# Graph layers with routed experts: the set-up taken by pairs of graphs, with identity products ahead of it on TensorE

## The chip, the cores and the metric

The kernel runs on one core of a Trainium2 chip. The metric is the device time of one execution, in microseconds (us); lower is better. The names of the engines are those of the profile: PE is TensorE, PEld its weight loads, DVE is VectorE, ACT is ScalarE, POOL is GpSimd; SPq and ACTq are the queues from which SyncE and ScalarE issue DMA transfers.

## What is computed

```python
# x: (128, 128, 256), adj: (128, 128, 128), float32: 128 graphs of 128 nodes
def gnn(X, A):                       # X = layernorm(x), A = adj
    Xw = X @ Wv + bv
    sj, si = Xw @ aw[:d, 0], Xw @ aw[d:, 0]
    e = leaky_relu(sj[:, None, :] + si[:, :, None] + ab[0], 0.2)
    alpha = A * exp(e)
    T = alpha / (alpha.sum(-1) + 1e-12)
    return relu(X @ Wk[0] + T @ (X @ Wk[1]) + T @ T @ (X @ Wk[2]) + bk.sum(0))
x = x + gnn(layernorm(x), adj)
x = x + experts(layernorm(x))        # top-1 of 16 experts, capacity 1228, times the route's probability
```

The kernel never forms `Xw`: it folds the attention vectors into the weights. `WvT` times `aw` gives two columns (`attention columns`) that stand beside `Wk[0]`, and `bv` times `aw` gives two constants. One product of a graph with the widened matrix then gives the first hop and both attention sums.

## The kernel before

One step of the main loop is a turn, and turn k works on graph k; the graphs come in batches of four (G = 4). All engines run the same turns, each with its own `slot_fn(it, k)` (POOL L472, ACT L597, DVE L771, PE L1296), written out by hand and tied together by semaphores. Work on other graphs is laid into a turn: the layer norm of the input leads (`LEAD_STATS` = 7: VectorE takes the statistics of graph k + 7 and the moments of graph k + 6; `LEAD_X0` = 2: GpSimd makes the normed graph k + 2; `LEAD_XT` = 1: TensorE transposes graph k + 1), and the residual sum, the routing and the storing lag by 2 to 10 turns. Later turns also carry tiles of the experts. Products are made in three parts of a split float32 (high by high, high by low, low by high), so each operand needs a rounded copy (`..h`, made by ACT with CAST) and a remainder (`..l`, made by DVE with a subtraction).

What a graph needs before its turn can run: statistics and moments (`st`, `mv`, DVE L913, L918), the negated mean and the variance plus epsilon (`nm`, `ve`, ACT L640, L641), the reciprocal root (`r`, POOL L479), the normed graph (`x0`, POOL L483), its transpose (`ps_xt`, PE L1321), its high part (`xth`, ACT L606) and its low part (`xtl`, DVE L810). Then PE multiplies it with `w12` (two hops, 512 columns, into `ps_z12`) and with `w0` (260 columns, the attention sums among them, into `ps_z0`). DVE adds the constants (`svs`, L839), PE spreads one column over the partitions (L1363), ACT takes two exponentials (`e`, L627, L628), DVE takes their maximum (`em`, L887), multiplies with the adjacency and divides (`al`, `ri`, `tm`), and PE transposes the result in the next turn (L1338).

The order of the set-up is this:

- SP issues the input of graphs 0 to 3 as one transfer of 512 KB (L371), then `WvT`, `aw`, `bv`, `ab` (L372 to L375, all on the semaphore `d_v`), and then the next inputs and constants. ACT issues `Wk`.
- DVE takes statistics and moments of graphs 0 to 3, spreads `bv` over a tile (`bvb`, L1216), makes the remainder of `w12` (`remainders`), the low part of graph 0, and then in `attention_columns` (L741) the columns, the constants, the high and low parts of `w0` and the vector `cvec` that `svs` adds. After that come the statistics of graphs 4 to 6 and turn 0, then `hop_biases` (L755).
- ACT forms `nm` and `ve` once per batch of four, and then the high part of `w12` (L699).
- POOL builds the constants (the identity `ident` at L460 among them) and runs its turns from -2 on.
- PE waits for `d_v`, makes the attention columns (L1287), runs turn -1 (the transposes of graph 0), makes the constants (L1481), signals both with one semaphore (`s_pe0`), and starts turn 0.

`fillers(n)` (L1486) issues n products of the identity with itself into a bank that nobody reads. Here it is called only between the last turns and the expert tiles that follow.

## Time and profile before

| | |
|---|---|
| Time of three runs, median (lowest to highest) | 757.88 us (757.74 to 757.92) |
| The profiled execution: its own time | 759.5 us |
| The profiled execution: span of the core in the trace | 757.7 us |
| Busy in that span: PE | 710.1 us (94%) |
| Busy in that span: DVE | 640.3 us (85%) |
| Busy in that span: ACT | 480.2 us (63%) |
| Busy in that span: POOL | 445.4 us (59%) |
| Mean granted clock of TensorE, as the records give it | 0.987 of full speed |

All durations of single instructions come from the profiled execution. Its time is 1.6 us above the median of the three runs; its span leaves out what lies around the instructions. A row of the timeline gives the start of an instruction in us from the span's start, its length, engine, line, operation, output and inputs, shape and number of instructions, and in brackets how long the engine had been idle and what ended the wait. The rows of PE overlap: the end of a product is modelled, so the rate of a stream is read from one start to the next.

### The profile page before, as it was taken

How to read it: one execution, taken by the hardware profiler on the slowest of the kernel's cores; microseconds unless marked ns; L12 is line 12 of the kernel's file. 1: busy time of each engine (PE TensorE's matmuls, PEld its weight loads, DVE VectorE, ACT ScalarE, POOL GpSimd, SP SyncE). 2: the span in 40 equal slices, each digit the busy share in tenths (PEclk: the TensorE clock that was granted, in tenths of full speed). 3: DMA queues.
4: the chain of work that ended last, by engine and by line, in shares of the span. 5: the costliest groups of instructions: out<-in, count | busy, mean ns of one | idle time of the engine just before them, and what ended most of it. 6: DMA issues, size and time to landing. Idle time of an engine off the chain costs nothing.

```text
span 757.7 us, 18479 instructions
## 1 busy us (share of the span) xinstructions
PE 710.1 (94%) x4815; PEld 628.7 (83%) x4815; DVE 640.3 (85%) x3101; ACT 480.2 (63%) x1506; POOL 445.4 (59%) x525
## 2 busy tenths in 40 slices
PE   4999999999999999999999999999999999958773
PEld 3888888789899998989998999999999989847662
DVE  4899999999889988989898899889898888776552
ACT  2567777666666666667666666666676676544551
POOL 4325555546666667666656666676666665665563
PEclk9999999999999999999999999999999999988997
DMA  9524444534443444444444433444443322354430
GB/s 271 143 78 135 128 130 154 166 105 148 150 128 122 131 152 155 144 151 148 135 132 152 134 117 124 149 149 143 142 141 125 117 91 85 102 156 134 122 95 1
DMA packets 92985, 100.12 MB, mean 132 GB/s; under 512 B 10379, under 2 KB 85192, under 8 KB 92882
## 3 DMA queue, kind: packets, MB, share of 16 engines
q1 hardware_dynamic: 76996, 65.96, 29.3%
q0 software_dynamic: 13008, 30.07, 10.8%
q10 hardware_dynamic: 2880, 2.92, 1.4%
q8 instruction: 43, 0.70, 0.4%
q14 instruction: 58, 0.48, 0.2%
HBM read 49.92 MB, written 54.72 MB: 138 GB/s over the span
## 4 chain that ended last, share of the span: by engine, by line
PE 85%; DVE 8%; issue 3%; another core or an unknown queue 1%; POOL 1%; DMA 1%; ACT 1%; POOLq 0%; DVEq 0%
PE ps_z12a L1291 11%; PE ps_z12b L1291 11%; PE ps_lgb L1291 9%; PE ps_z0b L1291 8%; PE ps_z0a L1291 8%; PE ps_lga L1402 5%; PE ps_z0a L1370 4%; PE ps_z0b L1370 4%; PE ps_xt L1321 4%; PE ps_z12b L1349 4%; PE ps_xt L1389 3%; PE ps_z12a L1349 3%; PE ps_lgb L1431 3%; PE ps_t L1363 2%; PE ps_t L1338 2%
## 5 line engine op out<-in xcount | busy, mean ns | idle before, releaser
L541 POOL DMA_INDIRECT out<-lent,tok x143 | 146.5, 1025 | 159.9 <-DVE lent L1203 136.4
L528 POOL DMA_INDIRECT rowbuf<-rows,idx x128 | 129.7, 1013 | 54.4 <-issue 30.3
L606 ACT CAST xth<-ps_xt 128x256 fp32r<-128x256 f32 x128 | 47.8, 373 | 110.7 <-PE ps_xt L1321 109.3
L483 POOL TENSOR_SCALAR x<-xin,nm,r 128x256 f32<-128x256 f32 x128 | 84.6, 661 | 26.0 <-PE ps_xt L1321 20.1
L681 ACT ACTIVATE x<-rin 128x256 f32<-128x256 f32 x143 | 86.9, 608 | 1.9 <-DMA rin<-rowbuf 1.8
L1402 PEld LDWEIGHTS ps_lga<-swc,xft 128*128 128x128 f32 x512 | 76.5, 190 | 10.7
L663 ACT ACTIVATE od<-rows,oc,oa 128x256 f32<-128x256 f32 x128 | 77.0, 602 | 0.0
L479 POOL TENSOR_TENSOR r<-ve,mhalf 128x4 f32<-128x4 f32 x32 | 33.2, 1038 | 62.3 <-ACT ve L641 61.8
L810 DVE TENSOR_TENSOR xtl<-ps_xt,xth 128x256 fp32r<-128x256 f32 x128 | 53.8, 421 | 17.7 <-ACT xft L655 15.0
L1402 PE MATMUL ps_lga<-swc,xft 128*128 128x16 f32 x512 | 65.6, 241 | 0.0
L887 DVE TENSOR_TENSOR em<-e 128x128 f32<-128x128 f32 x128 | 39.2, 306 | 26.1 <-ACT e L628 23.6
L627 ACT ACTIVATE e<-ps_t,svs 128x128 f32<-128x128 f32 x128 | 47.1, 368 | 21.1 <-PE ps_t L1363 18.6
L913 DVE BATCH_NORM_STATS2 st<-xin 128x6 f32<-128x256 f32 x128 | 53.2, 416 | 6.1 <-DMA xin<-in_x 6.0
L1291 PE MATMUL ps_z12b<-w12l,xth 128*128 128x512 f32 x128 | 58.1, 454 | 0.0
L1291 PE MATMUL ps_z12a<-w12l,xth 128*128 128x512 f32 x128 | 57.2, 447 | 0.0
L1291 PE MATMUL ps_lgb<-ewh,xth 128*128 x194 | 56.6, 373 | 0.2 <-issue 0.2
L933 DVE SCALAR_TENSOR_TENSOR rows<-hb,xin 128x256 f32<-128x256 f32 x128 | 55.1, 431 | 1.5
L938 DVE BATCH_NORM_STATS2 st<-rows 128x6 f32<-128x256 f32 x128 | 52.6, 411 | 0.0
L1189 DVE TENSOR_TENSOR xtl<-ps_lgb,xth 128x256 fp32r<-128x256 f32 x112 | 46.8, 418 | 6.5 <-ACT xth L687 2.2
L1321 PE MATMUL ps_xt<-ident,x 128*128 128x128 f32 x256 | 49.7, 277 | 0.7 <-POOL x L483 0.4
L655 ACT COPY xft<-ps_xt 128x256 f32<-128x256 f32 x128 | 48.4, 378 | 2.8 <-PE ps_xt L1389 2.8
L612 ACT COPY tt<-ps_t 128x128 f32<-128x128 f32 x128 | 34.1, 267 | 23.2 <-PE ps_t L1338 23.0
(209 smaller groups left out, 2383.7 us busy)
## 6 DMA issues: line engine op xcount, KB each, us to landing
rin<-rowbuf SPq DMA_DIRECT2D x143, 130.0 KB
xin<-in_x SPq DMA_DIRECT2D x32, 512.0 KB, 4.1
out<-od SPq DMA_DIRECT2D x32, 512.0 KB
ain<-in_adj SPq DMA_DIRECT2D x32, 256.0 KB, 4.5
ewr<-in_ewT SPq DMA_DIRECT2D x16, 256.0 KB, 2.7
out<-lent,tok POOLq DMA_INDIRECT x143
rowbuf<-rin ACTq DMA_DIRECT2D x1, 2080.0 KB, 11.5
rowbuf<-rows,idx POOLq DMA_INDIRECT x128
```

What stands on the lines that cost most here:

```text
L483: pool.tensor_scalar(x0[:, g % 2, :], xin[:, g % BODY, :], nm1[:, q, g % G:g % G + 1], r1[:, q, g % G:g % G + 1], ALU.add, ALU.mult).then_ ...
L528: pool.indirect_dma_start(out=rowbuf, out_offset=bass.IndirectOffsetOnAxis(ap=idx[:, i:i + 1], axis=0), in_=rows[:, r, :], in_offset=None, ...
L541: pool.indirect_dma_start(out=out.rearrange("g n d -> (g n) d"), out_offset=bass.IndirectOffsetOnAxis(ap=tok[:, i % RY:i % RY + 1], axis=0 ...
L663: act.activation(od[:, b2 * G + j, :], rows[:, g % BODY, 0:D], ACT.Identity, bias=oc[:, b2, j:j + 1], scale=oa[:, b2, j:j + 1]).then_inc(s ...
L681: act.activation(x0[:, xr(i), :], rin[:, i % RI, 0:D], ACT.Identity, bias=rin[:, i % RI, NMR:NMR + 1], scale=rin[:, i % RI, RSTD:RSTD + 1] ...
L810: dve.tensor_tensor(xtl[:, g % 2, :], ps_xt[:, 0:D], xth[:, g % 2, :].bitcast(F32), ALU.subtract).then_inc(s_x0l, 1)
L913: dve.bn_stats(st1[:, g % 2, :], xin[:, g % BODY, :]).then_inc(s_st1, 1)
L933: dve.scalar_tensor_tensor(rows[:, r, 0:D], hb[:, g % 2, :], 0.0, xin[:, r, :], ALU.max, ALU.add).then_inc(s_x1, 1)
L1291: return pe.matmul(psum_out, lhs_l if part == 2 else lhs_h, rhs_l if part == 1 else rhs_h, start=start, stop=stop, skip_group_check=True)
L1321: mm = pe.transpose(ps_xt[:, t * P:(t + 1) * P], x0[:, g % 2, t * P:(t + 1) * P], ident[:])
L1370: pe.matmul(ps_z0[d][:, 0:D], tt[:, d, :], z1[:, d, :], start=False, stop=True, skip_group_check=True).then_inc(s_tz1, 1)
L1402: mm = pe.matmul(ps_log[:, (b2 * G + j) * E:(b2 * G + j + 1) * E], xft[:, t * P:(t + 1) * P], swc[:, t, :], start=(t == 0), stop=(t == KT ...
```

## The change

The input of graphs 0 to 3 is loaded as two pairs of 256 KB, each with its own semaphore. ACT and POOL form the factors of graphs 0 and 1 as soon as these two have their moments (`first_moments`, `s_ve0`, `s_r0`), and those of graphs 2 and 3 later: on ACT they stand behind the high part of graph 0. TensorE first waits for the identity alone and issues 20 products of it with itself, into `ps_t`; then it waits for `d_v` and makes the attention columns, which it now signals by themselves. In its turn -1 it transposes graph 0, issues one more such product, and makes the first three of the products with `w12`, which stood in turn 0; the constants (`bvb` by `awt`) come behind that, into `ps_z0b`, with a semaphore of their own (`s_pe1`). DVE makes the columns and the high part of `w0` before the low part of graph 0, and its low part and the constants behind it (`attention_constants`). The statistics and moments of graphs 4 to 7 are no longer taken before turn 0 (4 to 6) and in turns 0 and 1 (moments of 6, statistics and moments of 7): turn 0 now takes both for graphs 4 and 5, turn 1 both for graphs 6 and 7, ahead of the statistics of graph 8 that turn 1 had before. From turn 2 on nothing is changed.

```diff
-            sp.dma_start(xin[:, 0:G, :], xd[0]).then_inc(d_x[0], 16)
+            sp.dma_start(xin[:, 0:2, :], xd[0][:, 0:2, :]).then_inc(d_pair0, 16)
+            sp.dma_start(xin[:, 2:G, :], xd[0][:, 2:G, :]).then_inc(d_x[0], 16)
...
@@ POOL, slot_fn @@
-                    if g % G == 0:
+                    if it * BODY + g == 0:
+                        pool.wait_ge(s_ve0, 1)
+                        pool.tensor_tensor(r1[:, 0, 0:2], ve1[:, 0, 0:2], mhalf[:, 0:2], ALU.pow).then_inc(s_r0, 1)
+                        pool.wait_ge(s_r0, 1)
+                    elif it * BODY + g == 2:
+                        pool.wait_ge(s_ve1, 1)
+                        pool.tensor_tensor(r1[:, 0, 2:G], ve1[:, 0, 2:G], mhalf[:, 2:G], ALU.pow).then_inc(s_r1, 1)
+                        pool.wait_ge(s_r1, 1)
+                    elif g % G == 0:
@@ ACT @@
-            for k in range(-LEAD_STATS, G - LEAD_STATS + 1):
-                slot_fn(0, k)
+            def first_moments(lo, signal):
+                act.wait_ge(s_mv1, lo + 2)
+                act.mul(nm1[:, 0, lo:lo + 2], mv1[:, lo:lo + 2, 0], -1.0)
+                act.add(ve1[:, 0, lo:lo + 2], mv1[:, lo:lo + 2, 1], EPS).then_inc(signal, 1)
+
+            first_moments(0, s_ve0)
             act.wait_ge(d_w12, 32)
             for kt in range(KT):
                 act.copy(w12h[:, kt, :], w12r[:, kt, :]).then_inc(s_wh, 1)
-            phase_a(act, slot_fn, G - LEAD_STATS + 1, 1)
+            slot_fn(0, -LEAD_XT)
+            first_moments(2, s_ve1)
+            phase_a(act, slot_fn, 0, 1)
@@ DVE, attention_columns @@
                 for kt in range(KT):
-                    dve.tensor_copy(w0r[:, kt, D:D + 2], ps_set[:, 2 * kt:2 * kt + 2])
-                link(dve.tensor_copy(cjs[:], ps_set[:, 2 * KT:2 * KT + 2]))
+                    two = dve.tensor_copy(w0r[:, kt, D:D + 2], ps_set[:, 2 * kt:2 * kt + 2])
+                link(two)
                 link(dve.tensor_scalar(w0r[:, :, D + 2], w0r[:, :, D + 1], SLOPE, None, ALU.mult))
                 link(dve.tensor_copy(w0h[:], w0r))
+
+            def attention_constants():
+
                 dve.tensor_tensor(w0l[:], w0r, w0h[:].bitcast(F32), ALU.subtract).then_inc(s_w0l, 1)
+                dve.wait_ge(s_pe1, 1)
+                link(dve.tensor_copy(cjs[:], ps_z0[1][:, 0:2]))
                 link(dve.tensor_tensor(csum[:, 0:1], cjs[:, 0:1], cjs[:, 1:2], ALU.add))
@@ DVE, slot_fn @@
                 g = k + LEAD_STATS - 1
-                if valid(it, g) and not G <= it * BODY + g < LEAD_STATS - 1:
+                if valid(it, g) and it * BODY + g > LEAD_STATS:
                     input_moments(it, g)
...
                 g = k + LEAD_STATS
-                if valid(it, g) and not G <= it * BODY + g < LEAD_STATS:
+                if it * BODY + k in (0, 1):
+                    for near in range(G + 2 * k, G + 2 * k + 2):
+                        input_stats(0, near)
+                        input_moments(0, near)
+                if valid(it, g) and it * BODY + g > LEAD_STATS:
                     input_stats(it, g)
@@ DVE, the set-up @@
-            for k in range(-LEAD_STATS, -LEAD_STATS + G + 1):
-                slot_fn(0, k)
+            for g in range(G):
+                input_stats(0, g)
+                input_moments(0, g)
+            remainders()
             dve.wait_ge(d_v, 16 * 4)
             for t in range(KT):
                 link(dve.tensor_scalar(bvb[:, t, :], onesf[:], bvt[:, t:t + 1], None, ALU.mult))
-            remainders()
-            for k in range(-LEAD_STATS + G + 1, 0):
-                slot_fn(0, k)
             attention_columns()
-            for g in range(G, LEAD_STATS):
-                input_stats(0, g)
-                if g < LEAD_STATS - 1:
-                    input_moments(0, g)
+            slot_fn(0, -LEAD_XT)
+            attention_constants()
             slot_fn(0, 0)
@@ PE, slot_fn @@
-                if valid(it, k):
-
-                    if it * BODY + k == 0:
-                        pe.wait_ge(s_wh, KT)
-                        pe.wait_ge(s_w12l, 1)
+                if it * BODY + k == -LEAD_XT:
+                    fillers(1, ps_t)
+                    pe.wait_ge(s_x0h, 1)
+                    pe.wait_ge(s_wh, KT)
+                    pe.wait_ge(s_w12l, 1)
+                if it * BODY + k == -LEAD_XT:
+                    c = 0
+                    times_w(ps_z12[0][:], w12h, w12l, PARTS[:3], False)
+                if valid(it, k) and it * BODY + k > 0:
                     if valid(it, k - 2):
@@ PE, the set-up @@
-            pe.wait_ge(d_v, 16 * 4)
-
-            for kt in range(KT):
-                for t in range(KT):
-                    pe.matmul(ps_set[:, 2 * kt:2 * kt + 2], wvt[:, t, kt * P:(kt + 1) * P], awt[:, :, t],
-                              start=(t == 0), stop=(t == KT - 1))
+            pe.wait_ge(s_id, 1)
+            fillers(20, ps_t)
+            pe.wait_ge(d_v, 16 * 4)
+            for kt in range(KT):
+                for t in range(KT):
+                    mm = pe.matmul(ps_set[:, 2 * kt:2 * kt + 2], wvt[:, t, kt * P:(kt + 1) * P], awt[:, :, t],
+                                   start=(t == 0), stop=(t == KT - 1))
+            mm.then_inc(s_pe0, 1)
             slot_fn(0, -LEAD_XT)
             pe.wait_ge(s_vc, KT)
             for t in range(KT):
-                mm = pe.matmul(ps_set[:, 2 * KT:2 * KT + 2], bvb[:, t, :], awt[:, :, t],
+                mm = pe.matmul(ps_z0[1][:, 0:2], bvb[:, t, :], awt[:, :, t],
                                start=(t == 0), stop=(t == KT - 1))
-            mm.then_inc(s_pe0, 1)
+            mm.then_inc(s_pe1, 1)
```

## Rows read from the trace of the kernel before

**Rows 1.** The page: busy time of the engines; the chain that ended last.

```profile
PE 710.1 (94%) x4815; PEld 628.7 (83%) x4815; DVE 640.3 (85%) x3101; ACT 480.2 (63%) x1506; POOL 445.4 (59%) x525
...
PE 85%; DVE 8%; issue 3%; another core or an unknown queue 1%; POOL 1%; DMA 1%; ACT 1%; POOLq 0%; DVEq 0%
```

**Rows 2.** Busy time in stretches: us, PE, PEld, DVE, ACT, POOL busy, PEclk, DMA share, GB/s.

```profile
9.30:21.50 12.20, 10.78 (x39) 8.96 (x40) 8.88 (x32) 3.44 (x10) 4.26 (x5) 1.00 0.97 291
...
36.60:640.00 603.40, 601.85 (x4130) 535.22 (x4128) 546.90 (x2734) 411.06 (x1327) 364.40 (x417) 1.00 0.42 133
```

**Rows 3.** Timeline of the set-up, every engine: start us, us, engine, line, tile.

```profile
2.11 0.28 POOL L460 TENSOR_SCALAR_AFFINE_SELECT ident<-onesf 128x128 f32<-128x128 f32 x1
...
3.15 0.51 SPq L375 DMA_DIRECT2D abt<-in_ab  x1
...
6.02 0.43 DVE L913 BATCH_NORM_STATS2 st<-xin 128x6 f32<-128x256 f32 x1 [6.02 <-DMA xin<-in_x]
...
7.33 0.39 DVE L913 BATCH_NORM_STATS2 st<-xin 128x6 f32<-128x256 f32 x1
...
8.72 0.20 ACT L640 ACTIVATE nm<-mv 128x4 f32<-128x4 f32 x1 [5.32 <-DVE mv L918]
...
9.33 1.87 PE L1287 MATMUL ps_lgb<-awt,lent 128*128 128x2 f32 x8 [9.33 <-DMA abt<-in_ab]
...
9.96 1.29 DVE L738 TENSOR_TENSOR w12l<-lent,w12h 128x512 fp32r<-128x512 f32 x2
...
11.65 0.69 PE L1321 MATMUL ps_xt<-ident,x 128*128 128x128 f32 x2 [0.45 <-POOL x L483]
...
12.78 0.42 DVE L810 TENSOR_TENSOR xtl<-ps_xt,xth 128x256 fp32r<-128x256 f32 x1 [1.53 <-ACT xth L606]
13.12 0.22 DVE L746 COPY lent_w<-ps_lgb 128x2 f32<-128x2 f32 x2
...
14.11 0.70 DVE L750 TENSOR_TENSOR w0l<-lent_w,w0h 128x520 fp32r<-128x520 f32 x1
...
15.03 0.64 PE L1291 MATMUL ps_z0a<-w0h,xth 128*128 128x260 f32 x2
...
15.47 0.43 DVE L913 BATCH_NORM_STATS2 st<-xin 128x6 f32<-128x256 f32 x1
...
17.41 0.15 DVE L839 TENSOR_TENSOR svs<-ps_z0a,cvec 128x4 f32<-128x4 f32 x1
```

**Rows 4.** The same timeline, turns 0 to 2.

```profile
18.79 0.29 DVE L887 TENSOR_TENSOR em<-e 128x128 f32<-128x128 f32 x1 [0.83 <-ACT e L628]
...
21.98 0.16 DVE L839 TENSOR_TENSOR svs<-ps_z0b,cvec 128x4 f32<-128x4 f32 x1 [0.72 <-PE ps_z0b L1291]
...
23.41 0.29 DVE L887 TENSOR_TENSOR em<-e 128x128 f32<-128x128 f32 x1 [0.49 <-ACT e L628]
...
25.27 0.51 PE L1291 MATMUL ps_z0a<-w0h,xth 128*128 128x260 f32 x2 [0.21 <-DVE hb L925]
```

**Rows 5.** DMA issues of the first 40 us: tile, queue, KB each, us to landing.

```profile
abt<-in_ab SPq DMA_DIRECT2D x1, 0.5 KB, 6.1
```

**Rows 6.** DMA issues of the whole run, on the page: the same columns.

```profile
ewr<-in_ewT SPq DMA_DIRECT2D x16, 256.0 KB, 2.7
```

**Rows 7.** TensorE's own timeline, in the steady turns and late in the kernel.

```profile
36.49 0.38 PE L1321 MATMUL ps_xt<-ident,x 128*128 128x128 f32 x2
...
661.56 1.28 PE L1489 MATMUL ps_z0a<-ident 128*128 128x128 f32 x10
...
696.79 0.51 PE L1291 MATMUL ps_z0a<-ewh,xth 128*128 x2 [1.86 <-DVE xtl L1189]
```

**Rows 8.** Busy time in stretches late in the kernel, columns as in Rows 2.

```profile
670.00:673.40 3.40, 2.98 (x14) 2.99 (x15) 2.93 (x13) 0.37 (x1) 2.62 (x3) 0.51 0.61 203
...
697.40:700.70 3.30, 3.30 (x18) 3.30 (x17) 1.53 (x5) 1.08 (x4) 1.86 (x2) 0.50 0.30 82
715.00:720.00 5.00, 3.38 (x25) 2.69 (x24) 2.67 (x10) 2.56 (x7) 2.60 (x4) 1.00 0.32 99
```

More of the change, by code:

```diff
@@ L207, in graph_then_experts @@
         d_w12 = sem("d_w12")
+        d_pair0 = sem("d_pair0")
+        s_id = sem("s_id")
+        s_ve0 = sem("s_ve0")
+        s_r0 = sem("s_r0")
+        s_pe1 = sem("s_pe1")
         d_w0 = sem("d_w0")
@@ L460, in _ @@
             pool.affine_select(ident[:], onesf[:], pattern=[[1, P]], compare_op=ALU.is_equal, fill=0.0,
-                               base=0, channel_multiplier=-1).then_inc(s_pc, 1)
+                               base=0, channel_multiplier=-1).then_inc(s_id, 1)
             pool.affine_select(before_bf[:], steps_bf[:], pattern=[[1, P]], compare_op=ALU.is_gt, fill=0.0,
@@ L565, in _ @@
             top_row = pool.to_reg(TOK - 1)
-            pool.wait_ge(s_pc, 12)
+            pool.wait_ge(s_pc, 11)
             phase_a(pool, slot_fn, -LEAD_X0, 1)
@@ L910, in input_stats @@
             def input_stats(it, g):
-                if g % G == 0:
+                if it * BODY + g == 0:
+                    dve.wait_ge(d_pair0, 16)
+                elif it * BODY + g == 2:
+                    dve.wait_ge(d_x[0], 16)
+                elif g % G == 0:
                     dve.wait_ge(d_x[g % BODY // G], 16 * it + 16 * (g // BODY) + 16)
@@ L1209, in tile @@
                 finish(i)
-            dve.wait_ge(s_pc, 12)
-            for k in range(-LEAD_STATS, -LEAD_STATS + G + 1):
-                slot_fn(0, k)
+            dve.wait_ge(s_pc, 11)
+            for g in range(G):
+                input_stats(0, g)
+                input_moments(0, g)
+            remainders()
             dve.wait_ge(d_v, 16 * 4)
@@ L1282, in _, with fillers @@
         def _(pe):
-            pe.wait_ge(d_v, 16 * 4)
-            for kt in range(KT):
-                for t in range(KT):
-                    pe.matmul(ps_set[:, 2 * kt:2 * kt + 2], wvt[:, t, kt * P:(kt + 1) * P], awt[:, :, t],
-                              start=(t == 0), stop=(t == KT - 1))
+            def fillers(n, bank):
+                for _ in range(n):
+                    pe.matmul(bank[:, 0:P], ident[:], ident[:], start=True, stop=True, skip_group_check=True)
             def product(psum_out, part, lhs_h, lhs_l, rhs_h, rhs_l, start=False, stop=False):
@@ L1474, in tile @@
                 if i == WOVEN:
-                    fillers(5)
+                    fillers(5, ps_z0[0])
                     counts(IT, G31, True)
+            pe.wait_ge(s_id, 1)
[6 more added lines that the diff above has]
+            mm.then_inc(s_pe0, 1)
             slot_fn(0, -LEAD_XT)
@@ L1480, in _ @@
             for t in range(KT):
-                mm = pe.matmul(ps_set[:, 2 * KT:2 * KT + 2], bvb[:, t, :], awt[:, :, t],
+                mm = pe.matmul(ps_z0[1][:, 0:2], bvb[:, t, :], awt[:, :, t],
                                start=(t == 0), stop=(t == KT - 1))
-            mm.then_inc(s_pe0, 1)
+            mm.then_inc(s_pe1, 1)
             phase_a(pe, slot_fn, 0, 1)
-            def fillers(n):
-                for _ in range(n):
-                    pe.matmul(ps_z0[0][:, 0:P], ident[:], ident[:], start=True, stop=True, skip_group_check=True)
             logits(IT, BODY - 2)
             pe.wait_ge(s_hb, B - 1)
-            fillers(3)
+            fillers(3, ps_z0[0])
             turned_rows(IT, BODY - 1)
             turn(WOVEN)
-            fillers(3)
+            fillers(3, ps_z0[0])
             turn(WOVEN + 1)
             logits(IT, BODY - 1)
-            fillers(1)
+            fillers(1, ps_z0[0])
             for i in range(WOVEN, NT):
```

## The prediction

> **What bounds the kernel now.** I read the page first: TensorE is busy for 94% of the span and carries 85% of the chain that ended last [rows 1]. The table of stretches shows where it is not: from 36.6 to 640 us it is busy 601.85 of 603.40 us, before that it waits [rows 2]. The steady turns are bound by TensorE, and the change does not touch them. What it can bring is the time by which they start earlier. So the mark for the sum is the first z0 product of turn 2, now at 25.27 us [rows 4]; from there on both kernels issue the same instructions.
>
> The timeline of the set-up shows two chains. The input lands and VectorE starts on it at 6.02; ScalarE begins the factors at 8.72, behind four graphs' statistics; the transposes of graph 0 start at 11.65. The other one starts with `d_v`: TensorE waits until 9.33 for `ab`, issued at 3.15 and landed 6.1 later, and makes the columns. VectorE copies them at 13.12 only, because the constants, behind graph 0, share their semaphore. The remainder of w0 ends at 14.81, z0 of turn 0 starts at 15.03, and `svs` comes at 17.41, behind statistics that began at 15.47 [rows 3, 5]. In turns 0 and 1 VectorE stood idle 0.83 and 0.49 us before `em` [rows 4].
>
> The clock is read with care. The stretch from 9.3 to 21.5 shows a grant of 1.00 [rows 2], yet two transposes take 0.69 us at 11.65 and 0.38 at 36.49 [rows 3, 7]. Late in the kernel the same ratio of durations stands beside grants of 0.50 and 1.00, that is 1.2 and 2.4 GHz [rows 7, 8]. I take it that the set-up ran at 1.2 GHz and the records simply begin later.
>
> **The change, part by part.**
>
> *Input in pairs.* A 256 KB load has landed in 2.7 us from its issue in the median of the whole run [rows 6], so pair 0 lands between 3.5 and the 5.92 of the whole; I take 4.8. Two graphs cost 7.33 - 6.02 = 1.31 us, and from ScalarE's start to the transposes it took 11.65 - 8.72 = 2.93 [rows 3]. Graph 0 is ready at 9.1, at 10.2 by the late end. Both are before TensorE has finished the columns (below), so this chain no longer sets anything. Its extra issue costs SP about 0.5 us (the length of L375) [rows 3], and delays everything behind it by 0 to 0.5: `d_v` comes between 9.3 and 9.8, I take 9.5. Graphs 2 and 3 get their factors on ScalarE behind graph 0's high part; that makes them ready near 13.5, needed near 14.8: nothing, and at most its excess if that cover goes.
>
> *Fillers.* Late in the kernel five of them (ten instructions) take 1.28 us at full grant, the last one's drawn-out end included [rows 7]; I take 0.22 each (0.26 with that end), and twice that, 0.44, at half. They start at 2.4, when `ident` is there [rows 3]. All at half: until 11.2. All at full: 6.8. After its waits TensorE worked at half from about 670 to 673.4 and from 697.4 to 700.7, some 3.3 us, and then at full [rows 8]. With 3.3 us at half, or 5.5 to allow for a later rise, 7.5 to 12.5 fillers are slow and the rest take 0.22: they end between 8.4 and 9.6. I take 9.2, within the wait for `d_v`: they cost nothing, and the columns start warm.
>
> *Weights.* VectorE now makes the remainders of w12 (1.29) before `bvb` (9.96 - 9.33 = 0.63) [rows 3], and must be through both when the columns come, at 10.45. Had ScalarE started on the high part at 8.72 as now, half of it 0.6 later, VectorE would be done at 11.2 and 0.75 would be paid. But ScalarE no longer stands behind four graphs, only two, and can start once the weights have landed; I take nothing.
>
> *Columns.* Eight products, 1.87 us now [rows 3], half of that at full clock: `s_pe0` at 10.45. VectorE's copies to the start of the remainder took 14.11 - 13.12 = 0.99, less 0.13 for the constants' copy that leaves this place; then the low part of graph 0 (0.42 and a semaphore, 0.5), then the remainder, 0.70 [rows 3]: 10.5 + 0.86 + 0.5 + 0.75 = 12.6. TensorE meanwhile does graph 0's transposes (high part ready at 11.3; they and the high part took 12.78 - 11.65 = 1.13 at half clock), one filler, three w12 products of 512 columns at 2.4 GHz (0.21 each), the constants and graph 1's transposes by 12.6. z0 starts at 12.8 instead of 15.03: 2.2 us earlier.
>
> *Constants and statistics.* Behind the remainder VectorE has the constants (15.47 - 14.81 = 0.66, and 0.2 for the copy moved here), the low part of graph 1 (0.45): 13.9, when the six z0 products are done too. `svs` at 13.95 instead of 17.41: 3.45 earlier, since the statistics of 4 to 6 no longer stand in front [rows 3].
>
> *Turn 0* takes statistics and moments of graphs 4 and 5, 1.31 us: 14.1 to 15.4. From the end of `svs` to `em` TensorE and ScalarE need at most 18.79 - 17.56 = 1.23, less than the statistics take now: `em` at 15.45 instead of 18.79, 3.35 gained [rows 3, 4]. *Turn 1*: the high part, `tm` and z0 are earlier by the same, and TensorE's stretch at half clock in front of z0 is gone; `svs`, now behind the low part of graph 2 and `hop_biases`, comes at 18.0 instead of 21.98, 4.0 gained. But now 1.31 for graphs 6 and 7 stand before `em`, in a turn that had 0.49 idle, and moments of one graph (0.18) leave: 1.31 - 0.18 with 0.1 for semaphores, less what of the idle time is free, 0.8 is given back. `em` at 20.2 instead of 23.41, z0 of turn 2 at 22.05: 3.2 us earlier. The wait of TensorE that this opens (about 1.1 us before the transpose of `tm`) is what is late next; its z0 products queue behind it, and VectorE waits for those.
>
> *Clock.* Transposes slowed and sped up with everything else: 0.69 against 0.38 [rows 3, 7]. The Trainium skill (TensorE: Matmul & The Clock Gate, Part 4: PE-mode transpose) says that full clock does not engage for transposes and that they do not count as busy in the same way. By it the three transposing steps on the path would keep their half-clock price, 0.3 us in all, and the sum would be 2.9; the trace disagrees with the first half.
>
> **Sum:** 3.2 us. The profiled execution spans 757.7 (its own time is 759.5, 1.6 above the median of the three runs); a difference carries over, 757.9 - 3.2 = 754.7.
>
> **Rivals.**
>
> *The clock falls back inside the set-up.* For it: the columns are 2 elements wide, turns 0 and 1 leave waits up to 1.1 us, and after a wait of 1.86 us the grant was 0.50 [rows 7, 8]. Against: from 715 to 720 TensorE was busy only 3.38 of 5.00 us and kept 1.00 [rows 8]. If it falls behind the columns, three w12 products cost 0.64 more, constants and transposes 0.4, of which 0.2 is slack, and z0 0.65: `svs` near 15.5, 1.9 gained, and some 0.4 of that is given back in turn 1: 756.4. The skill's sentence on transposes as not busy speaks for this one.
>
> *The fillers do nothing for the clock.* They are no real work and their widths are small. Then the columns end 0.93 later, and what follows up to `svs` costs some 1.9 more (as in the case before, with no slack left): 13.95 + 0.93 + 1.9 = 16.8, 0.6 gained, and turn 1 gives back 0.7: 758.0, no change.
>
> *Slower: the fillers outlast `d_v`.* Its place is the queue of TensorE ahead of the columns. At 0.44 each without a rise they end at 11.2, 1.7 us behind `d_v`, on top of the case before: 759.7. It decides from 0.35 us a filler on average, where 20 of them pass 9.5.
>
> *The tail takes its share.* Late in the kernel the grant falls after waits, and a stretch at half costs up to half of 3.3 us [rows 8]. Work shifted by 3 us may meet one fall more or one less: 756.4 or 753.1.
>
> **How the numbers follow.** The forecast has 0.52, the fall in the set-up 0.18, no effect on the clock 0.10, overrun 0.06, the tail 0.08 up and 0.06 down. A measurement of this kernel can tell about 0.2%, 1.5 us: faster means below 756.4. That takes the forecast, the better tail and half of the two cases that land on 756.4: 0.52 + 0.06 + 0.13 = 0.71; slower is the overrun, 0.06; the same 0.23. The unknown landings move the forecast by 0.4 either way. The range leaves out most of no effect and overrun above and part of the better tail below: 753.4 to 757.5.
>
> **What would show it.** Right: two pairs of inputs; fillers from 2.4 on, whose spacing halves on the way and whose last ends before the columns begin; columns in about 0.9 us; `svs` near 14.0 and 18.0; `em` of turn 1 waiting for nothing, directly behind statistics; z0 of turn 2 near 22.05; steady turns unchanged. Wrong: columns again in 1.9 us, products of 512 columns every 0.43 us before 18, fillers still running when `ab` lands, or a tail whose stretches at 0.50 have changed in number.

## The result, and the profile after

The changed kernel takes 755.39 us in the median of 6 runs (753.92 to 757.45), the kernel before 757.90 beside it (757.74 to 758.69). The recorded ratio is 0.9957, with a 95% interval from 0.9947 to 0.9968: faster by 0.3 to 0.5%, or 2.4 to 4.0 us. The quotient of the two medians alone is 0.9967, near the upper end of that interval. The forecast was 754.7 in a range from 753.4 to 757.5.

| | before | changed |
|---|---|---|
| Time, median of 6 runs | 757.90 us | 755.39 us |
| The profiled execution: its own time | 759.5 us | 753.94 us |
| Its span in the trace | 757.7 us | 752.2 us |
| Busy in it: PE | 710.1 us | 713.5 us |
| Mean granted clock | 0.987 | 0.988 |

The two profiled executions lie 5.5 us apart in span, twice as far as the medians: the one of before was slower than all six of its runs, the one of the changed kernel is almost the fastest of its own. So the traces are compared stretch by stretch and not by their ends.

The page of the changed kernel, the lines that answer to [rows 1]:

```profile
PE 713.5 (95%) x4857; PEld 632.3 (84%) x4857; DVE 641.0 (85%) x3101; ACT 479.5 (64%) x1508; POOL 444.8 (59%) x526
...
PE 86%; DVE 8%; issue 2%; POOL 1%; another core or an unknown queue 1%; ACT 0%; POOLq 0%; DVEq 0%
```

TensorE has 42 instructions more, the 21 identity products of two instructions each. Its busy time has grown by 3.4 us only, since the products of the set-up behind them are shorter, and its share of the chain is nearly what it was. The timeline of the set-up, the lines that answer to [rows 3, 4]:

```profile
2.44 7.30 PE L1316 MATMUL ps_t<-ident 128*128 128x128 f32 x40 [2.44 <-POOL ident L466]
...
4.68 0.43 DVE L946 BATCH_NORM_STATS2 st<-xin 128x6 f32<-128x256 f32 x1 [4.68 <-DMA xin<-in_x]
...
6.11 0.20 ACT L711 ACTIVATE nm<-mv 128x2 f32<-128x2 f32 x1 [2.75 <-DVE mv L951]
...
8.52 1.05 DVE L1251 TENSOR_SCALAR lent<-onesf,bvt 128x128 f32<-128x128 f32 x2
...
9.57 0.95 PE L1516 MATMUL ps_lgb<-awt,lent 128*128 128x2 f32 x8
...
10.38 0.42 PE L1350 MATMUL ps_xt<-ident,x 128*128 128x128 f32 x2
...
12.68 0.51 PE L1320 MATMUL ps_z0a<-w0h,xth 128*128 128x260 f32 x2
...
13.82 0.15 DVE L864 TENSOR_TENSOR svs<-ps_z0a,cvec 128x4 f32<-128x4 f32 x1
...
15.19 0.26 DVE L916 TENSOR_TENSOR em<-e 128x128 f32<-128x128 f32 x1
...
16.36 0.33 PE L1371 MATMUL ps_t<-ident,tm 128*128 128x128 f32 x1 [0.61 <-DVE tm L936]
...
17.54 0.15 DVE L864 TENSOR_TENSOR svs<-ps_z0b,cvec 128x4 f32<-128x4 f32 x1
17.60 0.42 DVE L946 BATCH_NORM_STATS2 st<-xin 128x6 f32<-128x256 f32 x1
...
19.21 0.41 DVE L906 TENSOR_TENSOR ewl<-ewr,ewh 128x256 fp32r<-128x256 f32 x1
...
19.54 0.29 DVE L916 TENSOR_TENSOR em<-e 128x128 f32<-128x128 f32 x1
...
21.39 0.51 PE L1320 MATMUL ps_z0a<-w0h,xth 128*128 128x260 f32 x2 [0.32 <-DVE hb L958]
```

The 20 identity products start at 2.44 and are 40 instructions. The first pair of graphs is there at 4.68 instead of 6.02, and ScalarE starts on its factors at 6.11 instead of 8.72. The columns take 0.95 us instead of 1.87. z0 of turn 0 starts at 12.68 (15.03 before), `svs` comes at 13.82 (17.41) and 17.54 (21.98), `em` at 15.19 (18.79) and 19.54 (23.41), and z0 of turn 2, the mark of the forecast, at 21.39 (25.27): 3.9 us earlier.

I split each traced execution in three: up to this mark, from there to the last transposes of an input graph, and the rest.

| execution | z0 of turn 2 | to the last transposes | the rest | span |
|---|---|---|---|---|
| before | 25.27 | 616.7 | 115.7 | 757.7 |
| changed | 21.39 | 616.6 | 114.2 | 752.2 |

Of the 5.5 us, 3.9 are the set-up, 0.1 the steady turns, and 1.5 the rest, in which the change touches nothing. Busy time by stretches late in the kernel, of before and then of the changed kernel (columns as in [rows 2]; the entry behind the five engines is the granted clock):

```profile
660.00:680.00 20.00, 11.13 (x73) 9.58 (x72) 13.65 (x69) 9.74 (x23) 13.66 (x15) 0.91 0.50 157
680.00:700.00 20.00, 16.04 (x98) 14.47 (x99) 12.67 (x42) 9.45 (x22) 10.90 (x11) 0.85 0.46 140
700.00:720.00 20.00, 15.81 (x113) 13.74 (x112) 11.52 (x39) 10.73 (x26) 11.38 (x13) 0.98 0.41 123
```

```profile
660.00:680.00 20.00, 11.48 (x62) 10.09 (x63) 14.49 (x58) 9.52 (x21) 12.47 (x13) 0.84 0.48 152
680.00:700.00 20.00, 16.04 (x115) 13.64 (x114) 11.39 (x41) 10.12 (x24) 11.52 (x12) 0.99 0.46 137
700.00:720.00 20.00, 16.14 (x110) 14.33 (x109) 11.26 (x38) 10.36 (x25) 11.41 (x13) 0.91 0.41 120
```

In both the grant is below 1.00 in parts of this stretch, but not in the same parts, and not to the same amount. Over the six runs of the changed kernel the longer times have the lower mean granted clock: 0.988 for the two of 753.9, 0.982 for the one of 757.45.

### The profile page after: what moved, and what is told of

The parts are those of the page before. It is cut to its first block, busy times and chain, and to the rows that moved or that the text cites. A ratio compares the mean times of both kernels' runs of the same rounds, so it can differ in the third digit from the quotient of the medians.

```text
span 752.2 us, 18567 instructions
## 1 busy us (share of the span) xinstructions
PE 713.5 (95%) x4857; PEld 632.3 (84%) x4857; DVE 641.0 (85%) x3101; ACT 479.5 (64%) x1508; POOL 444.8 (59%) x526
## 4 chain that ended last, share of the span: by engine, by line
PE 86%; DVE 8%; issue 2%; POOL 1%; another core or an unknown queue 1%; ACT 0%; POOLq 0%; DVEq 0%
PE ps_z12a L1320 11%; PE ps_z12b L1320 11%; PE ps_lgb L1320 9%; PE ps_z0a L1320 8%; PE ps_z0b L1320 7%; PE ps_lga L1435 5%; PE ps_z0a L1403 4%; PE ps_z0b L1403 4%; PE ps_z12b L1382 4%; PE ps_xt L1422 3%; PE ps_xt L1350 3%; PE ps_z12a L1382 3%; PE ps_lgb L1464 3%; PE ps_t L1396 2%; PE ps_t L1371 2%
## 5 line engine op out<-in xcount | busy, mean ns | idle before, releaser
L916 DVE TENSOR_TENSOR em<-e 128x128 f32<-128x128 f32 x128 | 37.4, 292 | 23.9 <-ACT e L642 20.9
```

## The experiments

Three groups of four kernels ran on three chips, one for each group, each beside runs of the kernel before on the same chip. The medians of the kernel before there are 758.90, 760.96 and 738.35 us, so times are compared inside a group only; the marks of the set-up can be compared across them, within the landing of the loads.

### First group: which part of the change pays

**Without the identity products** (`e1_no_identity`):

```diff
-            fillers(20, ps_t)
...
-                    fillers(1, ps_t)
```

> The changed kernel without its 21 identity products. Marks are read in the trace: the first svs (13.82 us in the changed kernel, 17.41 before) and the first z0 product of turn 2 (21.39 and 25.27). My theory, that the clock and the order each carry about half: TensorE makes the columns in 1.9 us again and stays at half clock until 18 to 21 us, svs near 16.5, z0 of turn 2 near 24.5 to 25, time about 3.3 us above the changed kernel's (around 758). Rival, that the new order does it alone: z0 of turn 2 below 22, no difference in the time beyond the spread of the tail (1.5 us).

Measured: 757.54 us in the median of 10 runs, ratio to before 0.9982 (0.9970 to 0.9994). Its timeline:

```profile
8.63 1.84 PE L1514 MATMUL ps_lgb<-awt,lent 128*128 128x2 f32 x8 [8.63 <-DMA abt<-in_ab]
...
15.63 0.16 DVE L864 TENSOR_TENSOR svs<-ps_z0a,cvec 128x4 f32<-128x4 f32 x1 [0.40 <-PE ps_z0a L1320]
...
23.25 0.51 PE L1320 MATMUL ps_z0a<-w0h,xth 128*128 128x260 f32 x2 [0.33 <-DVE hb L958]
```

The columns take 1.84 us again, and z0 of turn 2 comes at 23.25, 14.6 us after their start; in the changed kernel it is 11.8 us. So neither theory has it whole: in these traces the new order alone brings 2.0 of the 3.9 us, the identity products the other 1.9. My figure of 24.5 to 25 gave the order too little. The split hangs on when `ab` lands: here the columns began at 8.63, and in `e7_six`, below, a set-up that behaves like this one began them at 9.13 and had its mark at 23.77, by which the order brings 1.5.

**The identity products alone, in the kernel before** (`e2_identity_only`; the identity also gets a semaphore of its own, `s_id`):

```diff
+            pe.wait_ge(s_id, 1)
+            for _ in range(20):
+                pe.matmul(ps_t[:, 0:P], ident[:], ident[:], start=True, stop=True, skip_group_check=True)
             pe.wait_ge(d_v, 16 * 4)
```

> The kernel before with nothing but 20 identity products in front of the columns on TensorE. My theory: columns in 0.95 us and all products at full clock, but graph 0 still comes at 11.65 and VectorE still has the statistics of graphs 4 to 6 before svs: svs near 17.0 (17.41 before), z0 of turn 2 near 24.1 (25.27 before), time 1.1 us below before. Rival, that the clock is the whole gain: z0 of turn 2 near 21.5 and 3.5 us or more gained. Rival, that the products hurt by themselves: columns later than 9.6 us.

Measured: 758.57 us in the median of 10, ratio 0.9993 (0.9983 to 1.0004), no difference. Its timeline, and then its busy time by stretches with the granted clock:

```profile
2.44 6.41 PE L1286 MATMUL ps_t<-ident 128*128 128x128 f32 x40 [2.44 <-POOL ident L461]
...
8.69 0.95 PE L1291 MATMUL ps_lgb<-awt,lent 128*128 128x2 f32 x8
...
11.33 0.44 PE L1325 MATMUL ps_xt<-ident,x 128*128 128x128 f32 x2 [1.69 <-POOL x L484]
...
16.76 0.15 DVE L840 TENSOR_TENSOR svs<-ps_z0a,cvec 128x4 f32<-128x4 f32 x1
...
23.56 0.51 PE L1295 MATMUL ps_z0a<-w0h,xth 128*128 128x260 f32 x2 [0.23 <-DVE hb L926]
```

```profile
9.00:12.80 3.80, 1.53 (x13) 1.36 (x13) 1.97 (x7) 1.34 (x3) 3.07 (x4) 1.00 0.96 284
12.90:16.20 3.30, 3.30 (x12) 2.45 (x11) 2.84 (x11) 0.37 (x1) 1.07 (x1) 0.50 1.08 345
```

The columns are short, but TensorE then waits 1.69 us for graph 0, is busy for 1.53 of 3.80 us, and the grant falls to 0.50 from 12.9 to 16.2. z0 of turn 2 comes at 23.56, 1.7 us earlier than before. The products without the order bring a clock that is lost again behind the wait for graph 0. The mark is earlier all the same, by more than the 1.2 us that I expected, yet the times show no gain; the one traced execution of the kernel before may have had a late mark (see the end of the next part).

**The statistics back in front of turn 0** (`e3_stats_back`):

```diff
+            for g in range(G, LEAD_STATS):
+                input_stats(0, g)
+                if g < LEAD_STATS - 1:
+                    input_moments(0, g)
             slot_fn(0, 0)
...
-                if it * BODY + k in (0, 1):
-                    for near in range(G + 2 * k, G + 2 * k + 2):
-                        input_stats(0, near)
-                        input_moments(0, near)
-                if valid(it, g) and it * BODY + g > LEAD_STATS:
+                if valid(it, g) and not G <= it * BODY + g < LEAD_STATS:
```

> The changed kernel with the statistics of graphs 4 to 6 back in front of turn 0, all else as changed. My theory: svs of turn 0 some 1.8 us later (near 15.6), but turn 1 then has 1.1 us less to do before em, so z0 of turn 2 comes only 0.4 to 0.6 us later than 21.39: near 21.9. Rival, that moving the statistics is the main gain: z0 of turn 2 at 23 or later, time 1.7 us up.

Measured: 756.07 us in the median of 7, ratio 0.9965 (0.9954 to 0.9977). Its timeline:

```profile
8.91 1.05 PE L1516 MATMUL ps_lgb<-awt,lent 128*128 128x2 f32 x8 [0.21 <-DMA abt<-in_ab]
...
14.87 0.15 DVE L864 TENSOR_TENSOR svs<-ps_z0a,cvec 128x4 f32<-128x4 f32 x1
...
21.67 0.51 PE L1320 MATMUL ps_z0a<-w0h,xth 128*128 128x260 f32 x2 [0.22 <-DVE hb L954]
```

The number 21.67 looks like a hit and isn't one: here the columns start at 8.91, 0.66 us before those of the changed kernel. From the columns to z0 of turn 2 it takes 12.76 us against 11.82 (and 11.92 where the columns had to wait for `ab`, as they did here). Moving the statistics is worth 0.8 to 0.9 us, more than the 0.4 to 0.6 that I gave it and about half of what the rival did.

**One load for the four graphs** (`e4_one_load`):

```diff
-            sp.dma_start(xin[:, 0:2, :], xd[0][:, 0:2, :]).then_inc(d_pair0, 16)
-            sp.dma_start(xin[:, 2:G, :], xd[0][:, 2:G, :]).then_inc(d_x[0], 16)
+            sp.dma_start(xin[:, 0:G, :], xd[0]).then_inc(d_x[0], 16)
```

> The changed kernel with the input of graphs 0 to 3 in one load again, the factors still in pairs. My theory: graph 0 is ready before the columns are done in either case, so z0 of turn 2 stays within 0.3 us of 21.39 and the time within the spread. Rival, that the early pair is what pays: everything from the transposes on 1.3 us later, z0 of turn 2 near 22.7.

Measured: 755.35 us in the median of 9, ratio 0.9958 (0.9944 to 0.9972). Eight of the nine lie between 754.63 and 756.77; one took 1777.63 us, which nothing here explains, and the ratio leaves it out. Its timeline:

```profile
9.96 0.95 PE L1513 MATMUL ps_lgb<-awt,lent 128*128 128x2 f32 x8
...
21.78 0.51 PE L1317 MATMUL ps_z0a<-w0h,xth 128*128 128x260 f32 x2 [0.32 <-DVE hb L955]
```

From the columns to the mark it takes 11.82 us, the same as in the changed kernel to the hundredth. Loading by pairs brings nothing here; the 0.39 us by which the mark is later are all in the columns' start, 9.96 instead of 9.57. That start pointed to the next group: it does not follow the load, `ab` had landed at 8.6. Graph 0 was normed later than in the changed kernel (GpSimd began on it at 8.75 instead of 7.48), hidden behind these late columns. Whether the pairs pay where the columns begin a microsecond earlier, as in the next group, was not tried.

### Second group: how many products, and the late stretches

In the changed kernel VectorE saw `d_v` by 8.52, while TensorE began the columns at 9.57, without a wait, straight behind its products. So the products were late, by about one microsecond.

**14, 30 and 6 products instead of 20** (`e5_fourteen`, `e6_thirty`, `e7_six`):

```diff
-            fillers(20, ps_t)
+            fillers(14, ps_t)
```

and the same with 30 and with 6.

> The changed kernel with 14 identity products in front instead of 20. In the changed kernel VectorE saw d_v by 8.52 us, yet TensorE was in its 20 products until 9.46 and only then began the columns. My theory: 14 are over by 8.5 even at half clock, the columns start when d_v lands (8.5 to 8.9), and everything behind follows at the same distance, z0 of turn 2 some 11.8 us after the columns' start: 20.4 to 20.7, time about 0.8 us below the changed kernel's. Rival: TensorE needs the longer work for the clock, the columns take 1.9 us again and z0 of turn 2 comes near 23.

> The changed kernel with 30 identity products in front: the price of one, doubled the other way. My theory: ten more at full clock put the columns 2.2 us later, near 11.7, and z0 of turn 2 at 23.5, so the time comes 2.1 us above the changed kernel's. Rival, that the columns are not what the rest hangs on: less than half of that shows at turn 2.

> The changed kernel with 6 identity products in front, over at 5.1 us, so that TensorE waits 3.5 us before the columns. My theory: the clock does not rise before the columns or falls again in the wait, and the set-up runs like the one without identity products: columns 1.85 us, z0 of turn 2 14.6 us after their start (23.2). Rival, that any work early on is enough: z0 of turn 2 below 21.

Measured, with the kernel before at 760.96 in this group: 14 products 757.75 us (ratio 0.9958, 0.9931 to 0.9984), 30 products 759.13 (0.9977, 0.9965 to 0.9989), 6 products 759.59 (0.9983, 0.9966 to 1.0000). The timelines, 14 first, then 30, then 6:

```profile
2.44 5.37 PE L1316 MATMUL ps_t<-ident 128*128 128x128 f32 x28 [2.44 <-POOL ident L466]
...
8.69 1.05 PE L1516 MATMUL ps_lgb<-awt,lent 128*128 128x2 f32 x8 [0.88 <-DMA abt<-in_ab]
...
20.61 0.51 PE L1320 MATMUL ps_z0a<-w0h,xth 128*128 128x260 f32 x2 [0.33 <-DVE hb L958]
```

```profile
2.44 8.89 PE L1316 MATMUL ps_t<-ident 128*128 128x128 f32 x60 [2.44 <-POOL ident L466]
...
11.17 0.95 PE L1516 MATMUL ps_lgb<-awt,lent 128*128 128x2 f32 x8
...
22.99 0.51 PE L1320 MATMUL ps_z0a<-w0h,xth 128*128 128x260 f32 x2 [0.33 <-DVE hb L958]
```

```profile
2.44 2.93 PE L1316 MATMUL ps_t<-ident 128*128 128x128 f32 x12 [2.44 <-POOL ident L466]
...
9.13 1.87 PE L1516 MATMUL ps_lgb<-awt,lent 128*128 128x2 f32 x8 [3.76 <-DMA abt<-in_ab]
...
23.77 0.51 PE L1320 MATMUL ps_z0a<-w0h,xth 128*128 128x260 f32 x2 [0.32 <-DVE hb L958]
```

With 14, TensorE waits 0.88 us for `ab` and begins at 8.69; the columns are still short, and the mark is at 20.61, 0.8 us before the changed kernel's. The ratio of 0.9958 is that of the changed kernel on its chip (0.9957), so this group does not show the 0.8 us in the times. With 30, the columns start at 11.17 and the mark follows at the same distance of 11.82. Against the changed kernel's trace the ten more cost 1.6 us and not 2.2, since in this execution fewer of them ran slowly: by 0.44 and 0.22 us a product, 12.4 of the 20 were slow in the changed kernel and 9.7 of the 30 here. With 6, TensorE stands idle 3.76 us, the columns take 1.87, and the mark comes 14.64 us after them: the set-up of the kernel without products, to 0.02 us. So 6 products with a wait of 3.76 us behind them bring nothing, and 14 with 0.88 us keep the columns short.

**Products in the late waits** (`e8_tail_identity`):

```diff
+                if i == WOVEN + 2:
+                    fillers(12, ps_xt)
+                if i == WOVEN + 5:
+                    fillers(17, ps_xt)
```

> The changed kernel with 12 and 17 more identity products late in the kernel, in the two longest waits of TensorE there (3.1 and 4.1 us), into a bank that is free. My theory, that the spread of the times comes from stretches at half clock after such waits: the grant stays at 1.00 until 695, one or two stretches at 0.50 less, the time 1 to 1.5 us below the changed kernel's and the runs closer together. Rival, that those stretches are hidden behind VectorE: no gain. Rival, that the products come in the way: slower by up to 1 us.

Measured: 760.73 us in the median of 10, ratio 1.0012 (0.9994 to 1.0030), where the changed kernel without them had 0.9957 and the version with 14 products, on this chip, 0.9958. TensorE's timeline:

```profile
664.54 3.48 PE L1316 MATMUL ps_xt<-ident 128*128 128x128 f32 x24
...
677.27 5.03 PE L1316 MATMUL ps_xt<-ident 128*128 128x128 f32 x34
```

The expectation fell. The 12 took 3.48 us and the 17 took 5.03, 0.29 us each, more than I gave them, so that part of them ran at half clock and they outlasted the waits of 3.1 and 4.1 us that they were put in. In this trace the part behind the last transposes takes 121.3 us, against 114.2 to 118.0 in the nine others outside the third group. The runs show that the products cost time; that they do it by outlasting the waits is the reading of one trace. The same trace has a grant of 1.00 from 682.4 to 740 us, where the changed kernel's falls to 0.91 between 700 and 720, and TensorE still stood waiting for `xtl` of VectorE for 20.3 us in all, against 15.3. So here a clock that stayed up brought nothing. Whether it would pay without the delay stays open.

### Third group: the changed kernel against a better one

**The changed kernel again, and 14 products again** (`e11_changed_again`, `e12_fourteen_again`): the kernels are those of the result and of `e5_fourteen`, without any edit.

> The changed kernel as it is, once more, beside the three that follow. My theory splits a run in three: up to z0 of turn 2, from there to the last transposes of an input graph, and the rest. The first should be 21.0 to 21.8, 3.5 to 4.3 below the kernel before, the second within 1 us of the 616.7 that the kernel before took, and the spread of the times should lie in the third, as it did between the runs so far (114.2 to 118.0 us). Rival, that the gain is also lost somewhere else for good: the second part longer by 1 us or more than before in this run too.

> The version with 14 identity products again, now on the same chip as the changed kernel with its 20. My theory: z0 of turn 2 near 20.6, 0.4 to 1.2 us before that of the changed kernel, and the same difference in the median of the times, as far as the spread lets it be seen. Rival, that the shorter stretch leaves the clock lower in some executions: its times above those of the changed kernel.

Measured, with the kernel before at 738.35 (12 runs, 737.14 to 739.61): the changed kernel 735.25 in the median of 5 (734.90 to 736.25), ratio 0.9960 (0.9946 to 0.9975); with 14 products 734.19 (733.95 to 734.84), ratio 0.9945 (0.9932 to 0.9959). The slowest run with 14 is faster than the fastest of the changed kernel, by 0.06 us. The three parts of the changed kernel's trace are 20.96, 616.8 and 95.4 us: the first as expected, the second at its place, the third some 19 us shorter than in the traces of the other groups. The columns in the changed kernel's timeline, then the timeline with 14:

```profile
9.04 1.05 PE L1516 MATMUL ps_lgb<-awt,lent 128*128 128x2 f32 x8 [0.27 <-DMA abt<-in_ab]
```

```profile
8.59 1.05 PE L1516 MATMUL ps_lgb<-awt,lent 128*128 128x2 f32 x8
...
20.51 0.51 PE L1320 MATMUL ps_z0a<-w0h,xth 128*128 128x260 f32 x2 [0.32 <-DVE hb L958]
```

With 14 the mark is at 20.51, that of the changed kernel in this group at 20.96. But these 0.45 us are not the price of six products: in this execution the changed kernel was through with its 20 and waited 0.27 us for `ab`, which landed at 9.0. With 14 it had landed at 8.5, and the columns followed straight behind the products, all of which had run at half clock (6.15 us for 14, 0.44 each). The medians differ by 1.06 us, more than the marks. So the version with 14 products beats both kernels on this chip, but this pair of traces does not show by what.

**Columns that don't wait for `ab`, and the biases on GpSimd** (`e9_early_columns`, `e10_biases_on_pool`; the second is the first with one more edit):

```diff
-            sp.dma_start(bvt[:], bv).then_inc(d_v, 16)
+            sp.dma_start(bvt[:], bv).then_inc(d_vb, 16)
...
-            dve.wait_ge(d_v, 16 * 4)
-            for t in range(KT):
-                link(dve.tensor_scalar(bvb[:, t, :], onesf[:], bvt[:, t:t + 1], None, ALU.mult))
...
+            for t in range(KT):
+                act.activation(bvb[:, t, :], onesf[:], ACT.Identity, bias=cvec[:, 0:1],
+                               scale=bvt[:, t:t + 1]).then_inc(s_bvb, 1)
...
-            fillers(20, ps_t)
-            pe.wait_ge(d_v, 16 * 4)
+            fillers(12, ps_t)
+            pe.wait_ge(d_v, 16 * 2)
```

(the load of `ab` is moved to `d_vb` in the same way), and for the second besides, the two sums of `hop_biases` taken out of VectorE's queue:

```diff
-            hop_biases()
...
+                if it * BODY + k == 1:
+                    pool.wait_ge(d_bk, 16)
+                    pool.tensor_tensor(bias[:], bkr[:, 0, :], bkr[:, 1, :], ALU.add).then_inc(s_bias, 1)
+                    pool.wait_ge(s_bias, 1)
+                    pool.tensor_tensor(bias[:], bias[:], bkr[:, 2, :], ALU.add).then_inc(s_bias, 1)
```

> The changed kernel with 12 identity products, and the columns waiting for WvT and aw alone: bv and ab have their own semaphore, and the tile bvb is made by ScalarE in its idle time instead of VectorE. My theory: the columns hang on ab, the last of four small loads, without needing it; they start near 7.8, VectorE copies them when Wk[0] is there (8.7) and z0 of turn 2 comes at 19.8 to 20.2. Rival: with only 12 products the clock has not risen when the columns begin in an execution where it rises late, so z0 of turn 2 stays above 20.6.

> The version with early columns, and the sum of the hop biases made by GpSimd in its idle turn 1 instead of by VectorE between turns 0 and 1. My theory, that VectorE's queue sets turns 0 to 2 once the clock is up: 0.84 us of its work gone, z0 of turn 2 0.6 to 0.85 us earlier than in the version before it. Rival, that TensorE or the exponentials set these turns: less than 0.3 us. Rival, that GpSimd's sum comes too late for the first residual sum or slows VectorE: z0 of turn 2 later.

Measured: 735.47 in the median of 7 (733.49 to 737.17), ratio 0.9961 (0.9946 to 0.9976), and 735.25 in the median of 5 (734.30 to 736.35), ratio 0.9957 (0.9942 to 0.9971). The timeline of the first, and the busy time by stretches of the second:

```profile
8.08 1.09 PE L1521 MATMUL ps_lgb<-awt,lent 128*128 128x2 f32 x8
...
20.00 0.51 PE L1325 MATMUL ps_z0a<-w0h,xth 128*128 128x260 f32 x2 [0.33 <-DVE hb L966]
```

```profile
5.60:8.90 3.30, 2.26 (x20) 2.07 (x20) 2.41 (x7) 1.44 (x4) 2.28 (x3) 1.00 0.83 237
9.00:15.70 6.70, 6.15 (x23) 5.09 (x23) 3.90 (x15) 2.15 (x8) 3.57 (x6) 0.50 1.12 336
```

The profiled execution of the first does what was meant, its mark is at 20.00. The medians of the two do not differ beyond their spread, and neither is faster than the version with 14 products. The runs of the first fall into two kinds: two at 733.5 us with a mean grant of 0.993, five from 735.2 to 737.2 with 0.985 to 0.988. The trace of the second, a run of 736.35 us with 0.987, shows what such a run can look like: full clock until 8.9, TensorE waiting 1.04 us for `aw` with its 12 products over by 6.9, then 0.50 from 9.0 to 15.7 and the mark at 22.06. That is not the rival of a clock that rises late, but a clock that had risen and fell again. That the longer runs of the first are of this kind is likely from their grants, but no trace of one was taken. For the biases the answer holds for a start at half clock only: from `svs` to `svs` it took 3.68 us (14.52 to 18.20), against 3.77 in `e1_no_identity` (15.63 to 19.40), which also came to its first `svs` at half clock. 0.84 us less on VectorE gained 0.1 there. What it gains when the clock stays up was not seen.

## Why the prediction was right, and where it was not

**The mechanism.** What bounds the kernel was read rightly: from z0 of turn 2 to the last input graph's transposes the two traces differ by 0.1 us, and what the set-up gains arrives there whole. The mark moved by 3.9 us where 3.2 were forecast, the median by 2.5 where it was 3.2. That 754.7 and 755.39 lie so near each other is in part luck: the set-up brought 0.7 us more than forecast, and 1.4 us of it are not in the difference of the medians.

**Input in pairs.** The landing was put at 4.8 and the statistics began at 4.68; that the chain then sets nothing is shown by `e4_one_load`, for columns that begin as late as there.

**Fillers and `d_v`.** This step failed in its sizes. I took `d_v` at 9.5 and the products' end at 9.2, "within the wait for `d_v`: they cost nothing". In the changed kernel's trace `ab` had landed at 8.5, in spite of the extra issue, and the products lasted until the columns at 9.57: 0.36 us each, just past the 0.35 from which the prediction let the overrun decide. They cost about 1.0 us there. The overrun was in the list as a rival, but with a price only for the case that the clock does not rise at all; it happened in small with the clock risen. The two errors nearly cancelled, so that the columns began where the forecast had them, which is luck. How the step comes out changes from one execution to the next (landing as issue plus time to landing, us):

| execution | products | `ab` landed | columns start | what they waited for |
|---|---|---|---|---|
| changed | 20 | 8.5 | 9.57 | the products |
| `e4_one_load` | 20 | 8.6 | 9.96 | the products |
| `e8_tail_identity` | 20 | 8.5 | 9.21 | the products |
| `e3_stats_back` | 20 | 8.8 | 8.91 | `ab`, 0.21 us |
| `e11_changed_again` | 20 | 9.0 | 9.04 | `ab`, 0.27 us |
| `e5_fourteen` | 14 | 8.7 | 8.69 | `ab`, 0.88 us |
| `e12_fourteen_again` | 14 | 8.5 | 8.59 | the products |

So 20 products overran by 0.8 to 1.4 us in three traces and cost nothing in two, where the step held as forecast.

**Columns to `svs`.** 0.93 us forecast, 0.95 measured; z0 at 12.8 and 12.68, `svs` at 13.95 and 13.82.

**Turns 0 and 1.** `em` was put at 15.45 and came at 15.19; `svs` at 18.0 and 17.54; `em` of turn 1 at 20.2 and 19.54. The 0.7 us that the mark gained beyond the forecast come together here, step by step. I let turn 1 give back 0.8 us. From `svs` to `em` it went from 1.43 to 2.00 us, so 0.6 was given back. `e3_stats_back` says the same from the other side: the move of the statistics is worth 0.8 to 0.9 us where I expected 0.4 to 0.6. The wait that was to open before the transpose of `tm`, about 1.1 us, was 0.61 us in turn 0 and 0.34 in turn 1. As forecast, `em` of turn 1 has no idle time before it; directly in front of it stands `ewl`, a remainder of an expert's weights (L906, 19.21), which follows the statistics and was in that place before too.

**The clock in the set-up.** The prediction compared with late rows that it did not show, two transposes of the kernel before in a stretch at 0.51 and behind it, at 1.00:

```profile
672.07 0.63 PE L1431 MATMUL ps_z12a<-ident,x 128*128 128x128 f32 x2
...
673.78 0.38 PE L1431 MATMUL ps_z12b<-ident,x 128*128 128x128 f32 x2
```

That the set-up of before ran at 1.2 GHz although its stretches showed 1.00 is borne out by the columns, 1.87 and 0.95 us, and by the run without products. The rival that the clock falls back inside the set-up did not come true in the changed kernel's trace, where waits on the way were 0.24 to 0.61 us long. It did in `e2_identity_only` and in `e10_biases_on_pool`, so it is real. In both TensorE had waited first, 1.69 and 1.04 us. The Trainium skill's sentence on transposes (TensorE: Matmul & The Clock Gate, Part 4: PE-mode transpose) was weighed for it. These traces speak against its first half, that full clock does not engage for transposes: two transposes of the set-up take 0.42 us here, 0.69 before; what these two alone get shorter is about the 0.3 us that the prediction had for all three transposing steps. No run tests the second half, that they do not count as busy in the same way.

**The rest.** 1.4 of the 3.9 us are not in the difference of the medians, 2.5. That gap is not firm: the recorded ratio is worth 3.3 us, its interval reaches from 2.4 to 4.0, and three kernels with the same or nearly the same set-up lay 3.6 (`e4_one_load`), 3.2 (`e5_fourteen`) and 3.1 us (`e11_changed_again`) below the kernel before on their chips. The rival on the tail had this mechanism with 0.14 in all; it deserved more, since it is not one case beside the forecast but a spread on top of every case:

| execution | z0 of turn 2 | to the last transposes | the rest | span |
|---|---|---|---|---|
| `e1_no_identity` | 23.25 | 617.6 | 115.0 | 755.9 |
| `e2_identity_only` | 23.56 | 617.4 | 115.5 | 756.5 |
| `e3_stats_back` | 21.67 | 617.2 | 115.7 | 754.6 |
| `e4_one_load` | 21.78 | 616.8 | 114.4 | 753.0 |
| `e5_fourteen` | 20.61 | 617.0 | 117.3 | 754.9 |
| `e6_thirty` | 22.99 | 617.6 | 116.0 | 756.6 |
| `e7_six` | 23.77 | 617.2 | 118.0 | 759.0 |
| `e8_tail_identity` | 21.03 | 617.4 | 121.3 | 759.7 |
| `e11_changed_again` | 20.96 | 616.8 | 95.4 | 733.2 |
| `e12_fourteen_again` | 20.51 | 616.7 | 95.2 | 732.4 |
| `e9_early_columns` | 20.00 | 616.7 | 95.1 | 731.8 |
| `e10_biases_on_pool` | 22.06 | 617.1 | 95.4 | 734.6 |

With the two of the result's table and without `e8_tail_identity`, nine of these last parts, outside the third group, lie between 114.2 and 118.0 us, and the middle part spreads by 1 us as well. In most of these kernels the longer times went with a lower mean grant: with 6 products 758.3 to 759.2 us for 0.985 to 0.990, 759.9 to 762.7 for 0.978 to 0.984. So a gain of the set-up reaches the end, and is then seen through a spread of its own size. How much of the missing 1.4 us is chance and how much is lost for good late in the kernel stays open. Only one execution of the kernel before was traced, and it was longer than all six of its timed runs, so its own mark may usually be earlier than 25.27. Its `ab` (9.3) landed later than in all the others (8.4 to 9.1), but its first transposes waited for the input and not for `ab` [rows 3], so that this alone need not have moved the mark.

## What to carry to other kernels

Products that only warm TensorE's clock are free as long as they end before the awaited load; those that left 3.8 us of waiting behind them brought nothing. Count them by the row of the load and the time of one product at half clock, and look in more than one new trace whether the first real product still waits, since both the load and the clock's rise move by half a microsecond and more. Where a wait of 1.7 us followed, the clock fell again and the times showed no gain, so the order of the set-up is mended with them: in time, the order alone brought 1.4 us and the products alone 0.3, both together 2.5 to 3.6. A moved step is measured from the event that it hangs on, not from the start of the span; several marks here moved by half a microsecond because a load had landed earlier or later.

## What the runs showed of the hardware that was not expected

The same program takes different times on different chips: the changed kernel 755.39 us where the result was taken and 735.25 on the chip of the third group, the kernel before 757.90 to 760.96 elsewhere and 738.35 there. The set-up and the steady turns are equal to 0.5 us (20.96 and 616.8 against 21.39 and 616.6); nearly the whole difference is in the part behind the last input graph, 95.4 against 114.2 us. From 680 to 700 us TensorE is busy for 19.93 of 20 us on that chip, against 16.04 where the result was taken. `e11_changed_again` in this stretch, which stands above for the other two:

```profile
680.00:700.00 20.00, 19.93 (x146) 17.43 (x145) 15.67 (x49) 13.99 (x33) 14.86 (x16) 1.00 0.53 151
```

In the trace of the result VectorE stood idle for 1.66 us before the last step of a tile, at 690.78, although TensorE's last product of that tile had started at 688.80 and lasted 0.29 us. The one other thing that this step waits for in the program is the landing of an earlier scatter (the indirect store of a tile's rows). That the scatters land later where the result was taken would explain it, but it was not tried.

When the clock rises differs between executions of the same start: 14 products took 5.4 us in one and 6.3 in another, 20 between 6.3 and 7.7.
